# A fused cross-attention kernel: the order of value and score matmuls within a pair of steps

## The reference

```
scores = Q K^T / 4
feats  = [mean(scores), mean of row maxima, mean of var(softmax(scores))]   # per head
t      = exp(clip(MLP(feats)))          # two gelu layers of 64, then one output
attn   = softmax(Q K^T / (2 t))         # the second scores, with the learned temperature
out    = attn V ;  x = x + out Wo + bo
```

## Time and profile before

| what | value |
|---|---|
| median of 3 runs | 1465.39 us (1461.89 to 1470.97) |
| the profiled execution | 1467.12 us, span 1465.3 us |
| PE busy | 1256.8 us, 86% of the span |
| PE weight loads busy | 981.9 us, 67% |
| DVE busy | 933.0 us, 64% |
| ACT busy | 776.8 us, 53% |
| POOL busy | 166.0 us, 11% |
| mean granted TensorE clock | 0.803 of full speed |

### The profile page before, as it was taken

How to read it: one execution, slowest core, us unless ns; L and a number is a source line. 1 busy time by engine, 2 the same in 40 slices (tenths; PEclk the granted TensorE clock), 3 DMA queues, 4 the chain that set the end, 5 groups by cost and what they waited for, 6 DMA issues and landing times.

```text
span 1465.3 us, 40023 instructions
## 1 busy us (share of the span) xinstructions
PE 1256.8 (86%) x15060; PEld 981.9 (67%) x15060; DVE 933.0 (64%) x2355; ACT 776.8 (53%) x1771; POOL 166.0 (11%) x168
## 2 busy tenths in 40 slices
PE   2776889999999889989899989989998989897945
PEld 1644577868677776868586767777686858675732
DVE  2277756757685775767575777678575867674133
ACT  1233456757556564657465655656565756563210
POOL 0111010101011111111010201111111101000000
PEclk9656778979688896979698978989796979796655
DMA  2410000101010100101010101110010001000000
GB/s 79 134 43 21 19 23 18 40 23 38 11 33 26 33 18 18 32 25 26 17 31 20 38 11 33 26 27 24 22 30 25 26 17 37 5 3 1 9 0 4
DMA packets 46840, 39.08 MB, mean 27 GB/s; under 512 B 14577, under 2 KB 46001, under 8 KB 46641
## 3 DMA queue, kind: packets, MB, share of 16 engines
q1 hardware_dynamic: 46640, 36.41, 9.1%
HBM read 34.30 MB, written 2.10 MB: 25 GB/s over the span
## 4 chain that ended last, share of the span: by engine, by line
PE 69%; DVE 16%; ACT 7%; issue 6%; SPq 1%; ACTq 0%; POOL 0%; DVEq 0%; DMA 0%; POOLq 0%
PE pjp L523 12%; PE pjp L530 11%; PE s2p L573 11%; PE s1p L547 10%; PE pvp L590 8%; DVE est L1036 3%; PE tlp L674 2%; PE tlp L680 2%; PE s2p L563 2%; DVE negm L1030 2%; ACT pring L792 2%; PE tlp L696 2%; ACT kt L762 1%; PE tlp L624 1%; PE pjp L511 1%
## 5 line engine op out<-in xcount | busy, mean ns | idle before, releaser
L783 ACT ACTIVATE ering<-s1p,negm 128x400 f32<-128x400 f32 (+1 forms) x512 | 304.4, 596 | 204.9 <-DVE negm L1030 199.9
L1030 DVE TENSOR_REDUCE negm<-s1p 128x1 f32<-128x400 f32 (+1 forms) x512 | 289.3, 565 | 185.5 <-PE s1p L547 181.0
L792 ACT ACTIVATE pring<-s2p 128x512 f32<-128x512 f32 (+1 forms) x448 | 252.4, 566 | 161.8 <-PE s2p L573 161.4
L547 PE MATMUL s1p<-kt,qbd 32*128 32x400 f32 (+1 forms) x1024 | 304.1, 646 | 12.3 <-ACT ering L783 12.2
L1036 DVE BATCH_NORM_STATS2 est<-ering 128x6 f32<-128x400 f32 (+1 forms) x512 | 290.3, 567 | 0.9
L573 PE MATMUL s2p<-q2bd,kt 32*128 32x128 f32 (+1 forms) x3328 | 272.3, 294 | 0.0
L901 POOL TENSOR_TENSOR cr<-stage,cr 128x512 fp32r<-128x512 f32 x112 | 146.2, 1305 | 1010.2 <-ACT cr L774 1010.2
L573 PEld LDWEIGHTS s2p<-q2bd,kt 32*128 32x128 f32 (+1 forms) x3328 | 253.3, 201 | 7.3
L530 PE MATMUL pjp<-wkv,cr 128*128 128x256 f32 (+1 forms) x1248 | 212.4, 328 | 25.4 <-ACT kt L762 25.4
L523 PE MATMUL pjp<-cr,wkv 128*128 128x256 f32 (+1 forms) x1344 | 215.0, 317 | 21.2 <-DVE vt L1112 18.5
L523 PEld LDWEIGHTS pjp<-cr,wkv 128*128 128x128 f32 x1344 | 192.4, 218 | 49.4 <-issue 24.8
(11 more groups left out here) (171 smaller groups left out, 923.5 us busy)
## 6 DMA issues: line engine op xcount, KB each, us to landing
stage<-in_ctx SPq DMA_DIRECT2D x96, 256.0 KB, 2.8
qbd<-q_dram SPq DMA_DIRECT2D x128, 8.0 KB, 1.6
stage<-in_ctx SPq DMA_DIRECT2D x16, 65.0 KB, 2.0
vt<-in_x SPq DMA_DIRECT2D x1, 1024.0 KB, 5.5
q_dram<-late SPq DMA_DIRECT2D x1, 1024.0 KB, 4.9
late<-in_x SPq DMA_DIRECT2D x8, 128.0 KB, 2.2
out_y<-late SPq DMA_DIRECT2D x8, 128.0 KB, 1.7
late<-in_gate SPq DMA_DIRECT2D x1, 768.0 KB, 5.0
```

The lines of the kernel that those rows point to most:

```text
L547: nc.tensor.matmul(s1p[u % 3][:, 0:w], qbd[s.par][rows, g, :], kt[s.par][rows, g, lo:lo + w], start=True, stop=True).then_inc(s1_full, 1)
L783: nc.scalar.activation(ering[:, u % 3, 0:w], s1p[u % 3][:, 0:w], ACT.Exp, bias=negm[s.par][:, p, c:c + 1]).then_inc(s1_exp, 1)
L792: nc.scalar.activation(pring[0:m, v % NPR, 0:n], s2p[v % 2][0:m, 0:n], ACT.Exp).then_inc(s2_exp, 1)
L1030: nc.vector.tensor_reduce(negm[s.par][:, p, ch:ch + 1], s1p[u % 3][:, 0:w], AX.X, ALU.max, negate=True).then_inc(s1_max, 1)
```

## The change

In each even step the two `values` calls of the preceding pair move from behind `scores` and `scores2` to ahead of them. No instruction is added or removed, no wait changes, and no other engine's program is touched.

```diff
                     if step % 2 == 0:
+                        s_, v = s.second(step, 2)
+                        if s_.has(1, B) and v < S2U:
+                            values(s_, v)
+                            values(s_, v + 1)
                         if s.has(0, B - 1):
                             scores(s, step)
                             scores(s, step + 1)
                         s_, v = s.second(step, 0)
                         if s_.has(1, B) and v < S2U:
                             scores2(s_, (v, v + 1))
-                        s_, v = s.second(step, 2)
-                        if s_.has(1, B) and v < S2U:
-                            values(s_, v)
-                            values(s_, v + 1)
                     if step in plan:
                         project(s, *plan[step])
```

## The result

The changed kernel takes 1513.7 us in the median of 4 runs (1511.6 to 1527.4), against 1463.6 of the kernel before (4 runs, 1455.2 to 1471.0). The ratio is 1.036, interval 1.028 to 1.045: 3.6% slower. The profiled execution took 1514.6 us, its span is 1512.8 us, 47.5 longer than before, and the mean granted clock 0.801 against 0.803.

A forecast was written before the change was run, and what follows sets the result against it. PE's own program order was taken to set the pace, broken by waits for a chain over ACT and DVE. Terms summed to 43.5 us on the profiled 1467.1, 1510.6, so 1509 for the median; range 1480 to 1538.

The forecast's parts named there:

- slot 16: Slot without scores: the second values unit joins the loop, +0.3 to 0.5 us in some 10 pairs, 4 us.
- pairs with a projection: The projection covers the wait for the second-score exponential with 0.24 us of room left: no wait, cost nothing.
- steps 0 and 2: Step 0 has no projection and its group starts 0.58 us later: loss 0.29 us in 15 slots, 4.4 us.
- step 4: Scores come after the wait, delaying the gelu's table load and m1: 5.6 us in odd slots, 1.4 in even.
- steps 6 to 8: Late scores delay DVE's read of m2 and the exponential step 8's values need: 18.9 us odd, 7.7 even slots.
- steps 14 to 21: Even slots: step 14 gains 2.0 us; the stretch from step 16 with a tail starts 0.58 later, costing 3.5 us.
- the switch from projection to values: PE going from projection straight to values, 165 times: taken as nothing, bounded at 11.6 us up or down.
- now 0.29 + 1.34 = 1.63: Steps 0 and 2: PE's time from exponential E on, half the values plus scores and second scores, against 1.92 before.
- 8 odd slots: 18.9 us: The projection of step 8 starts 2.36 us later in odd slots, counted in full over 8 of them.
- the starts of slots have slack: Rival within 1%: a later wait, m3 or tail's first matmul, returns losses of steps 0 to 8; 1471 us, chance 0.10.
- Faster: the waits are E's own: Rival: E, a second-score exponential, is tied to other ACT and DVE work; 57 waits gain 0.29; 1449 us, chance 0.07.
- Faster still: the group is no longer torn: Rival: no wait separates scores from second scores (the group); 0.82 us back 57 times; 1419 us, chance 0.01.

The follow-up runs named there:

- the wait filled: New order at steps 0 and 2 only, others as before, step 2's waits filled with useless matmuls on 128 rows and 256 columns: 1444.1 us, ratio 0.991.
- unfilled: New order at steps 0 and 2 only, the order before at all other steps, nothing put into the waits: 1487.3 us, ratio 1.022.
- the edit to ACT: Changed kernel, with the temperature's exponential of step 8 moved behind the second-score exponential on ACT: 1512.6 us, ratio 1.039 to the kernel before.
- step 14 alone: New order in step 14 only, the order before at all other steps: 1458.7 us, ratio 1.005.
- the third order: Kernel before, with the values moved between scores and second scores in every pair: 1627.1 us, ratio 1.120.

## Why the prediction was right, point by point

The direction, the size and the place hold: 1509 was forecast, 1513.7 measured, and the loss lies in steps 0 to 8 and slot 16. But the terms of the sum are not all what I took them for, and that the total came out so close is luck. In us; a ratio is turned into us of 1460, which leaves each of these 5 to 12 us of uncertainty:

| term | predicted | measured |
|---|---|---|
| pairs with a projection | 0, bounds -11.6 to 11.6 | within the 4.7 below |
| steps 0 and 2 | 4.4 | 32 (2.2%) |
| step 4 | 7.0 | 10 (0.7%) |
| steps 6 to 8 | 26.6 | 11 (0.7%) for step 6; step 8 not told from 0 |
| steps 14 to 21 | 1.5 | with slot 16, 4.7 (0.3%) |
| slot 16 | 4 | 4.05 by its stage |

*Pairs with a projection.* The room of 0.24 us was enough. In 12 slots the stages of steps 21 to 31 are the same to 0.2 us in even slots and to 0.05 in odd ones, and the switch from projection to values has no price that shows. Around step 17, though, odd slots lose 0.5 us (3.64 to 4.15), which I had seen for even ones only.

*Steps 0 and 2, the step that failed, by size.* The chain was right: from the end of step 0's group to the start of PE's second values unit it is 796.32 - 793.40 = 2.92 us, and before to the second shift 783.07 - 780.32 = 2.75. The price was not. I let the first values unit run at once, and it waits 0.76 us, since no projection lies before it; that costs nothing by itself, as E sets the end, but it leaves PE idle. And "now 0.29 + 1.34 = 1.63" took the group at its full clock. It ran at half: 799.34 - 796.32 = 3.02. With the wait filled it is 686.80 - 685.10 = 1.70. The stage took 7.79 us before, where the clock was full, and takes 8.17 filled and 9.50 in the changed kernel: 0.4 us for the order and 1.3 for the clock. The runs with step 2 filled and unfilled show that the clock's part is the greater one, and that it doesn't end with the group: 3.1% lie between them, where a slower group accounts for at most 1.1 us in each of 15 slots, 1.1%. The rest lies behind it, mostly in steps 8 to 31 of even slots; why it lands there I did not test.

*Step 4.* The mechanism as forecast: scores after the wait, their exponential, table load, gelu, m1 at 2.94 after m0 instead of 1.85. In even slots the tail's transpose hides it: m0 to m1 went from 3.97 to 3.49.

*Steps 6 to 8.* The wait came as worked out, link by link. I had 2.36 us for odd slots from m1 on, and it is 0.16 + 2.33 = 2.49. What failed is "8 odd slots: 18.9 us", that it adds up in full: of the 1.45 us that the edit to ACT took off step 8, an odd slot kept 0.4. The rival "the starts of slots have slack" named the place where it comes back, the wait of the tail's first matmul for DVE, and I had argued it away since DVE's chain shifts too. It does shift; but the clock at which PE arrives there doesn't, and what follows is a long wait and a low clock, or the reverse. In even slots I predicted 1.1 and found 0.26 (0.16 and 0.10). The wait is there, 0.7 to 0.8 us, and at the half clock the stage takes 3.70 us (slot 8, 0.50); in the other even slots it took 2.61 to 2.75 at a granted clock of 0.94 to 0.99, where before it always ran at 0.50.

*The rivals.* "Faster: the waits are E's own" falls with steps 0 to 8, and step 14 alone showed nothing. "Faster still: the group is no longer torn" falls because the torn-off scores ran within the wait and kept the clock up too; that the overlap itself is worth 0.88 us a pair is shown by the third order. So the sum came out right because two errors offset each other: the clock in steps 0 and 2 left out, and step 8 counted in full. *Slot 16* took 4.05 us more, as forecast, but the granted clock there differs as well (0.68 before, 0.66 after), and its parts were not separated.

## What to carry to other kernels

In an in-order queue, put behind a wait only what nobody else needs early, and ahead of it whatever is ready: here two scores ahead of the wait fed DVE, hid the chain and kept PE busy. When a change makes PE wait longer, price the work after the wait at the lower clock too, and then look for the next wait that might return the loss before adding it up over all iterations; a loss in one place and its effect on the whole are two measurements. And where a wait can't be shortened, filling it with matmuls of full height can pay: here 3.1% against the same order unfilled, and 0.9% under the untouched kernel, with work that is thrown away.

## What the runs showed of the hardware

The clock fell though PE was busy without a gap: behind 4.68 of 4.68 us of busy PE, nearly all of it repeats of matmuls on 32 of 128 rows, the next 2.44 us ran at 0.50. A wait filled with 2.3 us of matmuls on 128 rows, PE busy for 2.98 of 3.29 us, was followed by 1.34 us at 1.00. A fully busy PE in the profile is thus no assurance of the full clock.

The length of a stage depends on the level at which it meets the clock, and slots of one run differ in it: the stage over steps 0 and 2 took 7.79 us (granted clock 1.00) to 9.30 us (0.82) in slots 3 to 14 of the kernel before, though each has the same 120 matmul records there, and 9.44 to 9.58 us in all of them after.
